# Layer 3 of a graph network kernel: the first power step's first two chunks run side by side, begun at the end of the feed forward, with new places for the edge products

## The reference

```python
h1 = _layernorm(x + gat_out, ln1_g, ln1_b)
ff = relu(h1 @ W1 + b1) @ W2 + b2
return _layernorm(h1 + ff, ln2_g, ln2_b)
...
# layer 3, h = relu(layernorm(x)), edges plus a loop on each node, K = 10, ALPHA = 0.1
msg = norm[:, None] * xk[src]
agg = segment_sum(msg, dst, num_segments=n_nodes)
xk  = (1.0 - ALPHA) * agg + ALPHA * h
...
x = x + relu(xK)
```

## Time and profile before

| what | value |
|---|---|
| median of 3 runs | 4969.4 us (4966.07 to 4975.6) |
| the profiled execution | 4971.43 us |
| its span | 4969.5 us |
| PE busy | 4197.7 us, 84% |
| POOL busy | 3260.7 us, 66% |
| DVE busy | 2560.9 us, 52% |
| ACT busy | 1034.5 us, 21% |
| mean granted clock of TensorE | 0.915 |
| L1988, dense products | 1080.6 + 1078.9 us, 9800 matmuls |
| L1034, gathers of layer 3 | 782.0 + 780.4 us, 1620 |
| adjacency loads | 290, 768 to 1088 KB each |

### The profile page before, as it was taken

How to read it: one execution, slowest core, us unless ns; L and a number is a source line. 1 busy time by engine, 2 the same in 40 slices (tenths; PEclk the granted TensorE clock), 3 DMA queues, 4 the chain that set the end, 5 groups by cost and what they waited for, 6 DMA issues and landing times.

```text
span 4969.5 us, 72321 instructions
## 1 busy us (share of the span) xinstructions
PE 4197.7 (84%) x25760; PEld 2695.7 (54%) x25760; DVE 2560.9 (52%) x8838; ACT 1034.5 (21%) x2922; POOL 3260.7 (66%) x3390
## 2 busy tenths in 40 slices
PE   3999588999985555667667999999999999999999
PEld 2776466766664555556554444444544444444444
DVE  7999545565554677778796222232232323222323
ACT  5887411111111001112224000000000000000101
POOL 2552377777775777777751767676766767676766
PEclk9999789999997667778778999999999999999999
DMA  5332322222222333333333666666666666666665
GB/s 150 113 111 97 86 66 70 71 66 70 71 70 70 94 96 95 96 95 95 88 78 105 204 190 204 198 202 201 205 199 199 204 196 208 196 203 198 202 200 165
DMA packets 455501, 686.46 MB, mean 138 GB/s; under 512 B 91793, under 2 KB 237879, under 8 KB 455120
## 3 DMA queue, kind: packets, MB, share of 16 engines
q1 hardware_dynamic: 341188, 454.71, 29.2%
q0 software_dynamic: 107584, 223.83, 17.2%
q10 hardware_dynamic: 6364, 3.20, 0.2%
HBM read 599.50 MB, written 82.31 MB: 137 GB/s over the span
## 4 chain that ended last, share of the span: by engine, by line
PE 31%; POOL 12%; DVE 6%; issue 5%; DMA 4%; ACT 1%; SPq 0%; POOLq 0%; DVEq 0%
PE ps L1988 26%; POOL arena L1034 10%; POOL E L999 2%; DVE B L2517 1%; DMA arena<-x_spill,src_i 1%; PE pt L2017 1%; DMA arena<-table,src_i 1%; PE ps L1810 1%; PE ps L2001 1%; PE pt L1827 1%; PE pt L1818 1%; DVE arena L2559 1%; DMA x_spill<-A 1%; DMA table<-E 0%; PE ps L1937 0%
## 5 line engine op out<-in xcount | busy, mean ns | idle before, releaser
L1988 PE MATMUL ps<-arena,E 128*128 128x512 fp8e4 (+1 forms) x4900 | 1080.6, 375 | 8.3 <-DVE C L2786 7.0
L1034 POOL DMA_INDIRECT arena<-table,src_i x810 | 782.0, 965 | 458.5 <-issue 233.6
L1988 PE MATMUL ps<-arena,A 128*128 128x512 fp8e4 (+1 forms) x4900 | 1078.9, 374 | 0.0
L1034 POOL DMA_INDIRECT arena<-x_spill,src_i x810 | 780.4, 963 | 348.6 <-issue 235.4
L984 POOL DMA_INDIRECT arena<-table,src_i x782 | 743.3, 950 | 346.9 <-issue 236.1
L999 POOL DMA_INDIRECT E<-gat_table,src_i x782 | 763.6, 976 | 269.8 <-issue 234.2
L1733 PE MATMUL ps<-E,arena 128*128 128x352 f32 (+22 forms) x2932 | 737.1, 403 | 118.4 <-DMA arena<-table,src_i 110.2
L1988 PEld LDWEIGHTS ps<-arena,E 128*128 128x128 f16 x4900 | 465.0, 98 | 507.3 <-issue 8.5
L1988 PEld LDWEIGHTS ps<-arena,A 128*128 128x128 f16 x4900 | 464.4, 98 | 495.7 <-issue 5.5
L2888 DVE SCALAR_TENSOR_TENSOR C<-ps,sc_b,scores 128x128 f32<-128x128 f32 x490 | 138.8, 345 | 1090.6 <-PE ps L2001 1089.0
L1733 PEld LDWEIGHTS ps<-E,arena 128*128 128x128 f32 x2932 | 491.2, 201 | 291.5 <-DMA arena<-table,src_i 141.0
(11 more groups left out here) (350 smaller groups left out, 4424.9 us busy)
## 6 DMA issues: line engine op xcount, KB each, us to landing
arena<-adj SPq DMA_DIRECT2D x180, 1024.0 KB
arena<-adj SPq DMA_DIRECT2D x90, 1088.0 KB
adj<-E SPq DMA_DIRECT2D x39, 784.0 KB, 3.7
arena<-table,src_i POOLq DMA_INDIRECT x1592
O<-dst_rows SPq DMA_DIRECT2D x112, 224.0 KB
arena<-adj SPq DMA_DIRECT2D x20, 768.0 KB
x_spill<-A SPq DMA_DIRECT2D x55, 256.0 KB, 2.5
arena<-x_spill,src_i POOLq DMA_INDIRECT x810
```

The lines of the kernel that those rows point to most:

```text
L1034: pool.indirect_dma_start(out=y_rows[:, g % ERING, k, :], out_offset=None, in_=(table, x_spill)[half], in_offset=bass.IndirectOffsetOnAxis ...
L1988: mm = pe.matmul(chunk_banks[n % 2][:, 0:len(some) * P], y[:, i, h * D:(h + 1) * D], adj_ring[:, piece % ADJ_RING, 0:len(some), at:at + P] ...
```

## The change

The first edit is in the plan. In step 0 the first two chunks are interleaved: source tiles 0 to 32 of chunk 0, then the same of chunk 1, then tiles 33 to 48 of chunk 0, then of chunk 1. The second is the place of the edge groups: 185 + 21 g in step 0, 145 + 21 g in step 1, 110 + 21 g in the others. Group 40 then stands at 1025, 985 and 950 of its step. The third: TensorE no longer awaits `ff2` before the first dense product, but before the first turn, and the first four loads are sent at three points: two when the product of group 5 is made, one when the last first-norm (`ln_a`) is made, one when the product of group 6 is made. For this the two `ff1_out` buffers change places. Pieces are numbered by their place in the plan, and `READ_UPTO` awaits the pooled tiles from source tile 39 on.

```diff
-TURN_LAG, STORE_LAG, EDGE_LAG, EDGE_LATE, EDGE_GAP = 10, 26, 84, 115, 22
+TURN_LAG, STORE_LAG, EDGE_LAGS, EDGE_GAP = 10, 26, (185, 145, 110), 21
...
-        ff1_out = [... for k in (0, NT * WL2)]
+        ff1_out = [... for k in (NT * WL2, 0)]
...
+                at = [base + chunk_at_cost(c) + 2 * i * len(chunk_nodes(c)) / CHUNK for i in range(NT)]
+                made_at = base + chunk_at_cost(c + 1)
+                if step == 0 and c < 2:
+                    late = PARTS3[-1][0]
+                    at = [2 * (c * late + i if i < late else late + c * (NT - late) + i) for i in range(NT)]
+                    made_at = at[-1] + 2
                 for i in range(NT):
-                    plan.append((base + chunk_at_cost(c) + 2 * i * len(chunk_nodes(c)) / CHUNK, 0, "dense", step, c, i))
+                    plan.append((at[i], 0, "dense", step, c, i))
...
-            first = base + (EDGE_LAG if step else EDGE_LATE)
+            first = base + EDGE_LAGS[min(step, len(EDGE_LAGS) - 1)]
...
+        part_of = {i: r for r, (first, last) in enumerate(PARTS3) for i in range(first, last)}
+        pieces = [(step * CHUNKS + what, part_of[i]) for kind, step, what, i in plan
+                  if kind == "dense" and i == PARTS3[part_of[i]][0]]
+        piece_at = {of: n for n, of in enumerate(pieces)}
...
-        READ_UPTO = {0: 32, 32: 36, 36: NT - 1, NT - 1: NT}
+        READ_UPTO = {0: 32, 32: 36, 36: DENSE, DENSE: NT - 2, NT - 2: NT}
...
-                    sp.wait_ge(sem("ff2_ps"), ff_done[b > 0])
-                    for n in range(ADJ_RING):
-                        load_adj(n)
+                    sp.wait_ge(sem("ff2_ps"), ff_done[0] - 1)
+                    load_adj(0)
+                    load_adj(1)
+                    sp.wait_ge(sem("ln_a"), PTN)
+                    load_adj(2)
+                    sp.wait_ge(sem("ff2_ps"), ff_done[0])
+                    load_adj(3)
...
-                pe.wait_ge(sem("ff2"), ff_done[b > 0])
+                if b:
+                    pe.wait_ge(sem("ff2"), ff_done[1])
...
+                            if t == 0:
+                                pe.wait_ge(sem("ff2"), ff_done[0])
```

More of the change, by code:

```diff
@@ L290, in build @@
                                .rearrange("p (t k) -> p t k", k=2) for k in range(2))
-        ff1_out = [arena[:, k:k + 4 * T7 * P].rearrange("p (c e) -> p c e", c=4) for k in (0, NT * WL2)]
+        ff1_out = [arena[:, k:k + 4 * T7 * P].rearrange("p (c e) -> p c e", c=4) for k in (NT * WL2, 0)]
         next_dst = bn[:, 0:1].bitcast(I32)
@@ L387, in build @@
             for c in range(CHUNKS):
-                for i in range(NT):
-                    plan.append((base + chunk_at_cost(c) + 2 * i * len(chunk_nodes(c)) / CHUNK, 0, "dense", step, c, i))
-                plan.append((base + chunk_at_cost(c + 1), -1, "copy", step, c, 0))
-                plan.append((base + chunk_at_cost(c + 1) + TURN_LAG, 1, "turn", step, c, 0))
-                plan.append((base + chunk_at_cost(c + 1) + STORE_LAG, 4, "store", step, c * CHUNK, chunk_nodes(c).stop))
-            first = base + (EDGE_LAG if step else EDGE_LATE)
+                at = [base + chunk_at_cost(c) + 2 * i * len(chunk_nodes(c)) / CHUNK for i in range(NT)]
[4 more added lines that the diff above has]
+                    made_at = at[-1] + 2
+                for i in range(NT):
+                    plan.append((at[i], 0, "dense", step, c, i))
+                plan.append((made_at, -1, "copy", step, c, 0))
+                plan.append((made_at + TURN_LAG, 1, "turn", step, c, 0))
+                plan.append((made_at + STORE_LAG, 4, "store", step, c * CHUNK, chunk_nodes(c).stop))
+            first = base + EDGE_LAGS[min(step, len(EDGE_LAGS) - 1)]
             for g in range(EGROUPS):
@@ L401, in build, with inner_pieces @@
         plan = [entry[2:] for entry in sorted(plan, key=lambda entry: entry[:2])]
+        part_of = {i: r for r, (first, last) in enumerate(PARTS3) for i in range(first, last)}
+        pieces = [(step * CHUNKS + what, part_of[i]) for kind, step, what, i in plan
+                  if kind == "dense" and i == PARTS3[part_of[i]][0]]
+        piece_at = {of: n for n, of in enumerate(pieces)}
+        assert pieces == [(step * CHUNKS + what, part_of[i]) for kind, step, what, i in plan
+                          if kind == "dense" and i + 1 == PARTS3[part_of[i]][1]]
+        def inner_pieces(n):
+            return sum(r < len(PARTS3) - 1 for _, r in pieces[:n + 1])
         turns = [(step, what) for kind, step, what, _ in plan if kind == "turn"]
@@ L758, in after_l2 @@
                     ring_u8 = adj_ring.bitcast(U8)
-                    pieces = len(PARTS3) * CHUNKS
                     def load_adj(n):
-                        c, r = divmod(n % pieces, len(PARTS3))
-                        some, (first, last) = chunk_nodes(c), PARTS3[r]
+                        c, r = pieces[n]
+                        some, (first, last) = chunk_nodes(c % CHUNKS), PARTS3[r]
                         sp.dma_start(ring_u8[:, n % ADJ_RING, 0:len(some), 0:(last - first) * P],
@@ L777, in after_l2 @@
                         if kind == "dense":
-                            r = [last for _, last in PARTS3].index(i + 1) if i + 1 in [last for _, last in PARTS3] else None
-                            n = step * CHUNKS + what
-                            if r is None or n * len(PARTS3) + r + ADJ_RING >= STEPS * pieces:
+                            n, r = step * CHUNKS + what, part_of[i]
+                            at = piece_at[n, r]
+                            if i + 1 != PARTS3[r][1] or at + ADJ_RING >= len(pieces):
                                 continue
@@ L784, in after_l2 @@
                             else:
-                                sp.wait_ge(sem("piece_used"), n * (len(PARTS3) - 1) + r + 1)
-                            load_adj(n * len(PARTS3) + r + ADJ_RING)
+                                sp.wait_ge(sem("piece_used"), inner_pieces(at))
+                            load_adj(at + ADJ_RING)
                         if kind == "store":
@@ L799, in after_l2 @@
                     for u in range(ADJ_RING):
-                        sp.wait_ge(sem(f"adj_in{u}"), 16 * len(range(u, STEPS * pieces, ADJ_RING)))
+                        sp.wait_ge(sem(f"adj_in{u}"), 16 * len(range(u, len(pieces), ADJ_RING)))
                     sp.wait_ge(sem("y_out0"), 16 * STORES * (STEPS // 2 - 1) + 16 * PTN)
@@ L1976, in after_l2 @@
                             some, y = chunk_nodes(what), halves((E, A)[step % 2])
-                            r = [i < last for _, last in PARTS3].index(True)
-                            piece, at = n * len(PARTS3) + r, (i - PARTS3[r][0]) * P
+                            r = part_of[i]
+                            piece, at = piece_at[n, r], (i - PARTS3[r][0]) * P
                             if i == PARTS3[r][0]:
```

## The result

| | before | changed |
|---|---|---|
| median | 4970.28 us (4 runs, 4966.07 to 4975.6) | 4926.24 us (4 runs, 4923.41 to 4933.9) |
| ratio | | 0.9913, interval 0.9896 to 0.993 |
| profiled execution, its span | 4971.43, 4969.5 | 4933.9, 4932.0 |
| last feed forward product ends | 2679.6 | 2681.3 |
| from there to the last dense matmul's start | 2278.0 | 2240.0 |

The forecast was 4930, with a range of 4916 to 4957. P and S are, as in the prediction, the start of a step's dense work on TensorE and of its first gather on GpSimd; P1 and S1 are those of step 1. The length of step 9 is taken to the last dense matmul's start.

What follows compares the result with a forecast made beforehand. Layer 3's steps were held bound by gathers, started late by the previous step's last pooled store. Step 3 starts at 3365.2; plus 7 x 222.0 gives 4919.2; plus a 10.8 tail, 4930.0 us; range 4916 to 4957.

Steps and rivals of the forecast that it cites:

- S1: First GpSimd gather of step 1: 8.0 us after step 0's last edge group at 2924.9, so at 2932.9.
- wait at tile 33: Step 0, chunk 0: TensorE newly waits 7.2 us (5 to 10) for matrix piece 4, loaded behind the seven table stores.
- tail: From the last dense matmul to the kernel's end: 10.8 us instead of 11.6, VectorE and ScalarE having two tiles less.
- the hand-over: Last stores of a step to next step's first gather: from step 3 on, 7.75 us after dense work starts, not 14.6.
- early start: Start of layer 3: without the ff2 wait TensorE begins 7.0 us earlier, at 2679.65; most of this is not kept.
- the prediction's own sign: Step 1's first gather: the sum is wrong if it does not come within 3 us of 2933.
- late steps: Steps 3 to 9, edge lag 110 and gap 21: 222.0 us each, against 225.4 before.
- the gathers' loop: Steps 3 to 9: gathers, landing and next first gather bound the step, 216.3 + landing, 219.1 to 221.9 us.
- rival B: TensorE is the bound in every late step, 221.2 us each; kernel time 4921; chance 0.12.
- C: Hand-over gain half lost, stores or last gathers landing beside loads; loop 224 to 225.5, time 4951; chance 0.18.
- D: Only the place of the waits changes, hand-over stays at 14.6 us; time 4965 to 4972; chance 0.06.
- E: Slower: the narrower gap outruns the gathers, average landing over 10.8 us; 4978 at 12 us; chance 0.06.

Runs made afterwards that it cites:

- e1: Kernel before with only the new edge-group places (185, 145, 110 + 21 g) and their READ_UPTO, ff2 wait and loads as before: ratio 0.9931 to the kernel before.
- e2: Changed kernel with the old edge-group places (115 + 22 g in step 0, 84 + 22 g later), early start kept: ratio 1.001 to the kernel before.
- e4: Kernel before with pooled chunks' stores 15 units behind their last group instead of 26, edge groups unmoved: ratio 0.9916 to the kernel before.
- e3: Changed kernel with 184 in place of 185 in step 0: ratio 0.9909 to the kernel before, layer 3 2229.9 us.

## Why the prediction was right

By its steps, the profiled execution against the sum. All points of the changed kernel lie 1.5 us later from the start on, since the layers before ended so.

| point | sum | measured |
|---|---|---|
| dense work starts | 2679.65 | 2681.12 |
| wait at tile 33 | 7.2 | 7.33 |
| P1 | 2909.0 | 2912.2 |
| S0 | 2713.6 | 2715.2 |
| S1 | 2932.9 | 2943.3 |
| P2, S2 | 3137.8, 3152.5 | 3148.0, 3162.5 |
| P3 | 3365.2 | 3375.1 |
| mean of steps 3 to 9 | 222.0 | 220.9 |
| last dense matmul | 4919.2 | 4921.3 |
| tail | 10.8 | 10.7 |

The mechanism was the forecast's: the hand-over. It was forecast that the early start would mostly not be kept and that the gain would come of the last store getting ahead of the load at tile 16; e1, e2 and the run with the ff2 wait show the first, e4 the second. The new wait for piece 4 came where and as long as it was put. P1 is 1.7 us late beyond the 1.5 of offset, about the 2.0 us that two groups of step 0 wait for their rows, which the sum had not. By the prediction's own sign, S1 within 3 us of 2933, the sum is wrong in one step; with it step 1 lasts 235.8 us where about 228 was put, while steps 2 (227.1) and 3 to 9 and the place of their waits are as put.

**The step that failed: S1.** The sum gave 8.0 us from the last edge group of step 0 to the first gather; it was 14.3 (2929.05 to 2943.31): 6.5 to the store's issue and 7.7 from there, where the sum had 5.1 and 2.9. I had counted which load stands before which store for the late steps and not for step 0. The last store of step 0 has the cost 185 + 840 + 26 = 1051, the load at tile 48 of step 1's first chunk 955 + 96 = 1051, and the load goes first at equal cost. So S1 is 8.9 us late beyond the 1.5 us of offset: 6.3 from this, 2.6 because the last group itself came later than put. P2, S2 and P3 are each 8 to 9 us late with it: the sums of the following steps were right from there (S1 to S2 219.2, sum 219.6; S2 to P3 212.6, sum 212.7). e3 takes that collision away and has S1 - S0 of 219.1, where the sum has 219.3.

**The term that was mis-sized: the late steps.** 222.0 against 220.9, 7 x 1.1 = 7.7 us. I held the gathers' loop to be the bound: 202.3 + landing + 5.1 + 1.1 + 7.75. Three of its terms came out otherwise. From the first gather to that of group 39's last tile a late step mostly takes 200.0 to 200.1 us (202.5 to its last gather, where the step that I had read has 204.8); why the run is shorter is not shown. S - P is 8.4, since the tenth chunk's store is sent 5.5 us into the step (3595.48 to 3600.96) and not 4.85. And where TensorE still waits, at the last groups of steps 5 to 8, the landings in the chain that ended last are 6.3 to 7.4 us, not 5.6, as in step 7 (the chain, then the timeline of TensorE):

```profile
4462.19 7.42 DMA arena<-x_spill,src_i
```

```profile
4469.66 0.36 PE L2039 MATMUL pt<-rows,arena 128*128 128x26 f16 x8 [0.91 <-DMA arena<-x_spill,src_i]
```

(In the kernel before, too, the chain has landings up to 6.9 us; the prediction put its longest near 6.) The loop of step 7 is 195.0 us to that group's last gather, 7.4 of landing, 10.6 to the next step's start and 8.4 to the next first gather, together the 221.5 that this step lasts. Steps 3 and 4 have no wait and last 220.4 each: there TensorE itself is the bound, and with 2.7 us of waits in seven steps it nearly is in the others. That is rival B's picture for the late steps, its price 221.2. The two errors of the sum, +8.4 up to P3 and -7.7 behind it, nearly cancel, and this is why it came out 2 us from the profile's span and 4 from the median. The right time owes something to luck; the right sign and size do not.

The Trainium skill's fit of 2.0 us plus the bytes (DMA: Bandwidth & Descriptors, Anatomy of one DMA — SWDGE (gpsimd) path) was set against this loop. By it TensorE had to be the bound of the late steps, and there it nearly is. That doesn't bear out the figure: the landings on record are 6.3 to 7.4 us there, and the margin came from the shorter run of gathers.

The tail went as put: from the last edge group to the last store's issue 5.6 us before and 5.5 here, with the last store sent 4.6 us after the last dense matmul instead of 5.8.

```profile
4920.38 0.26 PE L2039 MATMUL pt<-rows,arena 128*128 128x26 f16 x4
...
4925.93 0.38 SPq L814 DMA_DIRECT2D out_x<-X  x1
```

The clock after the wait at tile 33: 44 matmuls took 11.79 us, of which 0.4 is the last one's length; the 43 steps between their starts take 9.3 us at 0.216 each, so 2.1 us were lost, with 1.8 in the sum. The Trainium skill (TensorE: Matmul & The Clock Gate, Part 1: The HAM clock gate) has TensorE at half its clock after idleness, and the rows agree: 0.50 granted from 2717 to 2720 after 7.33 us of idleness, 1.00 from 2723.

Of the rivals C, D and E none has a trace of its own: stores landed early, S - P moved, and the waits at the end of the late steps stay under 1 us.

**A version beyond both.** By its one profile on the first chip the kernel with 184 has the shortest layer 3, 48.1 us under before and 10.1 under the changed one. Against the changed kernel on the same chip it was timed once, on the third chip, with medians 20 us apart and intervals that overlap. e4 gets 42.3 of these 48.1 us with a single number in the plan and nothing else of the change.

## What to carry to other kernels

When a step's gathers begin at the landing of its last store, look in the queue that sends the store for what stands before it at that moment: a megabyte load in front made the store's landing 3 to 5 us longer here, in the kernel before in each step, and its place was one number in a sorted plan. Compare the costs of the two entries for equality too. An earlier start on one engine is worth nothing while another engine's chain (here VectorE's last layer norm and its store) releases what comes next, here the load of piece 4 and the first gathers; undo each half of a double change alone before crediting it.

## What was not expected of the hardware

The changed kernel took 4926, 6194 and 6241 us in three measurements, the last two on different chips, each beside a kernel before that was as slow there. Of the 1243 us more in the second one's profile 757 lie before layer 3, and nothing here explains those. In the late steps, between 4300 and 6100 us, the granted clock of TensorE was 0.94 and 0.93 on these two chips, where it is 1.00 in the late steps of the first profile. On the second chip that stretch gives, as an estimate, 236 us of TensorE busy in a step of 270, where the first profile has 220.5 of 220.9: of the 49 us that a step takes longer some 15 are slower work and 34 idleness, which the trace gives mostly as issue, on TensorE and ScalarE alike. A gain of 0.9% from a shorter wait was not to be seen there (0.999 and 1.000).
